# A two-attention transformer layer on one core: batches in two halves through all head pairs, with norms and FFN in portions between attention steps

## The reference, cut to what matters

```
x = x + attn_a(layernorm(x))   # 16 heads of 128, q/k/v with biases, causal softmax, w_o, b_o
x = x + ffn(layernorm(x))      # per-row int8 quantisation, one 256x256 product, scale, bias, fp16
x = x + attn_b(layernorm(x))   # 16 heads: rope on q and k, 64 slots (s, cumulative logsumexp z),
                               # ok, softmax, W2, o; rms norm, gate g*sigmoid(g), Wo
x = x + ffn(layernorm(x))      # the same FFN weights again
```

## Time and profile before

| | |
|---|---|
| median of 3 runs | 817.05 us |
| the profiled execution, its own time | 818.15 us |
| its span, first to last instruction | 816.3 us |
| granted TensorE clock, mean | 0.989 |
| TensorE busy | 783.3 us (96%) |
| VectorE / ScalarE / GpSimd busy | 579.9 / 434.7 / 285.6 us |
| read from HBM | 22.45 MB |

### The profile page before, as it was taken

One profiled execution on the slowest core, in us unless ns is written; L12 is line 12 of the kernel. 1 busy time (PEld: TensorE's weight loads), 2 busy tenths in 40 slices (PEclk: granted clock), 3 DMA queues, 4 the chain that ended last, 5 costly groups with the idle time before them and its releaser, 6 DMA issues.

```text
span 816.3 us, 14609 instructions
## 1 busy us (share of the span) xinstructions
PE 783.3 (96%) x4628; PEld 665.2 (81%) x4628; DVE 579.9 (71%) x1502; ACT 434.7 (53%) x1188; POOL 285.6 (35%) x291
## 2 busy tenths in 40 slices
PE   8999999999999996899999999999999999999975
PEld 6788888888888885578888888888888888888863
DVE  4455555545554558878887888798888788887786
ACT  3555565555546452465556466556565665665421
POOL 7211010202101004444536346355364463563222
PEclk9999999999999999999999999999999999999998
DMA  7010101101010100100101001001001010000001
GB/s 241 25 53 12 39 13 39 48 3 51 5 46 13 51 1 14 53 1 14 53 0 50 14 13 51 0 13 51 0 14 51 6 58 0 13 0 1 1 1 52
DMA packets 23654, 23.76 MB, mean 29 GB/s; under 512 B 2369, under 2 KB 23361, under 8 KB 23506
## 3 DMA queue, kind: packets, MB, share of 16 engines
q1 hardware_dynamic: 23634, 23.51, 9.0%
HBM read 22.45 MB, written 1.05 MB: 29 GB/s over the span
## 4 chain that ended last, share of the span: by engine, by line
PE 88%; DVE 7%; POOL 2%; ACT 1%; issue 1%; DMA 1%; SPq 0%; POOLq 0%; DVEq 0%; ACTq 0%
PE ps L1282 21%; PE ps L1494 11%; PE ps L1391 7%; PE ps L1289 5%; PE ps L1312 5%; PE ps L1355 3%; PE ps L1396 3%; PE ps L1506 3%; PE ps L1331 3%; PE ps L1531 3%; PE ps L1518 2%; PE ps L1548 2%; PE ps L1550 2%; PE ps L1549 2%; PE ps L1519 2%; PE ps L1520 2%
## 5 line engine op out<-in xcount | busy, mean ns | idle before, releaser
L1282 PE MATMUL ps<-xT_hi,w_hi 128*128 128x512 f32 x256 | 109.6, 428 | 2.4 <-DVE rot L1013 1.5
L1282 PE MATMUL ps<-xT_hi,w_lo 128*128 128x512 f32 x256 | 100.9, 394 | 0.0
L1282 PE MATMUL ps<-xT_lo,w_hi 128*128 128x512 f32 x256 | 100.7, 393 | 0.0
L1043 DVE TENSOR_TENSOR wt<-ps,const 128x384 f32<-128x384 f32 x128 | 68.2, 554 | 40.3 <-PE ps L1507 20.4
L384 POOL TENSOR_TENSOR w_lo<-w_raw,w_hi 128x512 fp32r<-128x512 f32 x32 | 40.8, 1284 | 157.2 <-ACT w_hi L536 155.5
L440 POOL TENSOR_TENSOR rot_s<-rot_s,const 128x512 f32<-128x512 f32 x64 | 81.9, 1291 | 20.0 <-ACT rot_s L679 20.0
L581 ACT ACTIVATE wt<-wt,negmax 128x128 f32<-128x128 f32 (+1 forms) x128 | 56.7, 444 | 28.2 <-DVE negmax L907 28.2
L895 DVE TENSOR_TENSOR v<-ps,bv_b 128x256 f32<-128x256 f32 x64 | 27.0, 422 | 51.9 <-PE ps L1289 51.9
L698 ACT ACTIVATE v<-ps 128x256 f32<-128x256 f32 x64 | 24.4, 381 | 72.5 <-PE ps L1494 72.3
L1032 DVE RECIPROCAL enz<-zs 128x128 f32<-128x128 f32 x64 | 60.3, 943 | 1.0 <-ACT zs L685 1.0
L1282 PEld LDWEIGHTS ps<-xT_hi,w_hi 128*128 128x128 f32 x256 | 48.7, 190 | 12.2 <-issue 3.5
(11 more groups left out here) (174 smaller groups left out, 2264.4 us busy)
## 6 DMA issues: line engine op xcount, KB each, us to landing
w_raw<-a_w_q SPq DMA_DIRECT2D x8, 256.0 KB, 2.5
w_raw<-a_w_k SPq DMA_DIRECT2D x8, 256.0 KB, 3.3
wv<-a_w_v SPq DMA_DIRECT2D x8, 256.0 KB, 3.4
wo<-a_w_o SPq DMA_DIRECT2D x8, 256.0 KB, 2.6
w_raw<-b_Wq SPq DMA_DIRECT2D x8, 256.0 KB, 2.5
w_raw<-b_Wk SPq DMA_DIRECT2D x8, 256.0 KB, 3.4
wc<-b_Wv SPq DMA_DIRECT2D x8, 256.0 KB, 3.4
wc<-b_Wg SPq DMA_DIRECT2D x8, 256.0 KB, 3.9
```

What stands on the lines that cost most here:

```text
L1043: d.tensor_tensor(dst, src[:, 0:384], tri3, ALU.mult).then_inc(done, 1)
L1282: ins = mm(PJ[n[0]], w[:, m, c, h * P:(h + 1) * P], x[:, c, cols], start=(t == 0), stop=(t == len(terms) - 1))
```

## The change

A phase is now half `phase // 8`, pair `phase % 8`, 16 phases (`PHASES`) of two steps each: all eight pairs for batches 0 and 1, then all eight for batches 2 and 3, in both attentions. Everything is written out; no hardware loop is left. Each pair's weights are loaded and split twice, once per half.

Attention a's second half (steps 17 to 24) carries, in portions called `middle(0, r)`, the whole passage between the attentions for batches 0 and 1. Attention b's first half (steps 1 to 8) carries the same for batches 2 and 3 (`middle(1, x)`), and its second half (steps 17 to 21) the second FFN of batches 0 and 1 (`closing`). The last phase of attention a has attention b's first tasks in place of its own next ones. All portions use bank 7, which the output groups use too; `middle_done` holds the next group until the portion has left the bank. A half's projection sums are all kept in `accT` and turned back by `sum_rows`; only the last two batches of b still use `out_proj`.

The core of the diff (each engine has its share of the portions):

```diff
+PHASES = 2 * PAIRS
+LAST = 2 * PHASES - 1
-        ffns = [Ffn("f0_", (0, 1, 6, 7)), Ffn("f1_", (0, 1, 0, 1))]
+        ffns = [Ffn("f0_", (7, 7, 7, 7)), Ffn("f1_", (7, 7, 0, 1))]
 # SyncE
-            with sp.Fori(1, PAIRS) as i:
-                sp.wait_ge(a.w_lo, a.splits * i)
-                load_qk(a, a_wq, a_wk, cols)
-                load_v(cols)
-                sp.wait_ge(a.wo_lo, i)
-                load_o(a, a_wo, cols)
+            for phase in range(2, PHASES):
+                sp.wait_ge(a.w_lo, 3 * (phase - 1) + 2)
+                load_qk(a, a_wq, a_wk, columns(phase))
+                sp.wait_ge(a.w_lo, 3 * (phase - 1) + 3)
+                load_v(columns(phase))
+                sp.wait_ge(a.wo_lo, phase - 1)
+                load_o(a, a_wo, columns(phase - 1))
...
 # GpSimd, start-up
             pool.wait_ge(norms[0].xn, 4)
             split_tail(a, 0, 0)
+            split_tail(a, 0, 1)
+            split_tail(a, 0, 2)
             ln_rsqrt(0, 2)
             ln_rsqrt(0, 3)
-            pool.wait_ge(norms[0].xn, TILES)
-            split_tail(a, 0, 1)
-            split_tail(a, 0, 2)
...
 # VectorE
+            def middle(half, r, place):
+                b = 2 * half
+                if r == 1 and place == 0:
+                    add_rows(a, b)
+                if r == 1 and place == 1:
+                    add_rows(a, b + 1)
+                if r == 1 and place == 2:
+                    ln_stats(1, b, a.fin_acc, b + 1)
+                    ln_stats(1, b + 1, a.fin_acc, b + 2)
+                if r == 2 and place == 0:
+                    ln_scale(1, b)
+                    ln_scale(1, b + 1)
+                if r == 2 and place == 2:
+                    ffn_quant(0, b)
+                    ffn_quant(0, b + 1)
+                if r == 4 and place == 0:
+                    ffn_out(0, b)
+                if r == 4 and place == 1:
+                    ffn_out(0, b + 1)
...
 # TensorE
+            def sum_rows(ph, b):
+                for t in range(2):
+                    tile = slice((2 * b + t) * P, (2 * b + t + 1) * P)
+                    for c in range(C):
+                        o = t * D + c * P
+                        ins = tr(Y_[:, o:o + P], accT[:, c, tile], ident)
+                ins.then_inc(ph.fin_ps, 1)
+            def middle(half, r, place):
+                if r in (3, 4, 6, 7, 8) and place == 0:
+                    pe.wait_ge(ph.y_acc, groups)
+                if r == 1 and place == 0:
+                    pe.wait_ge(a.y_acc, PHASES * (half + 1))
+                    sum_rows(a, b)
...
+                if r == 3 and place == 0:
+                    ffn_transpose(0, b)
+                    ffn_transpose(0, b + 1)
+                if r == 4 and place == 0:
+                    pe.wait_ge(ffns[0].qT, b + 2)
+                    ffn_product(0, b)
...
+            def a_step(x):
+                a_turn(x, 0)
+                a_task(ahead, o)
+                middle(0, r, 0)
+                a_turn(x, 1)
+                a_task(ahead, o + 1)
+                a_scores(x + 1)
+                middle(0, r, 1)
+                a_values(x)
+                a_task(ahead, o + 2)
+                if x % 2 == 1:
+                    a_task(ahead, o + 3)
+                middle_done(0, r)
...
-            ffn_product(0, 1)
-            keep_busy(4, oT_hi[:, 0, 0, :], 15)
-            transpose_x(1, 0, ffns[0].banks[0])
-            transpose_x(1, 1, ffns[0].banks[1])
-            s1_product(0)
-            s1_product(1)
-            ffn_transpose(0, 2)
...
+            x = LAST - 1
+            a_turn(x, 0)
+            b_task(0, "s")
+            a_turn(x, 1)
+            b_task(0, "q0")
+            a_scores(x + 1)
+            b_task(0, "q1")
+            a_values(x)
+            b_task(0, "z")
+            b_task(0, "k0")
+            out_group(a, x)
+            b_task(0, "k1")
...
+            for x in range(2 * PHASES):
+                b_step(x)
```

More of the change, by code:

```diff
@@ L240, in layer_kernel, with half_of, pair_of, task @@
         block = ctx.enter_context(nc.Block())
[L242 to L275, removed]
-            return bank, before + 1
-        def before_in_bank(h, j):
-            order = [(g, k) for g in (h - 1, h) for k in range(NB) if (g, k) < (h, j)]
-            return [(g, k) for g, k in order if B_BANKS[g % 2][k] == B_BANKS[h % 2][j]][-1]
+        def half_of(phase):
+            return phase // PAIRS
+        def pair_of(phase):
+            return phase % PAIRS
+        def task(phase, f):
+            n = NA * phase + f
+            return n % 2, n // 2
+        def evacuated(phase, f):
+            bank, before = task(phase, f)
+            return bank, before + 1
+        def banks_of(phase):
+            return B_FIRST if phase == 0 else B_BANKS[phase % 2]
+        def slot(phase, j):
+            bank = banks_of(phase)[j]
+            before = sum(banks_of(p).count(bank) for p in range(phase))
+            return bank, before + banks_of(phase)[:j].count(bank)
+        def slot_ps(phase, j):
+            return NB * phase + j + 1
+        def slot_done(phase, j):
+            bank, before = slot(phase, j)
+            return bank, before + 1
+        def before_in_bank(phase, j):
+            order = [(p, k) for p in range(phase + 1) for k in range(NB) if (p, k) < (phase, j)]
+            return [(p, k) for p, k in order if banks_of(p)[k] == banks_of(phase)[j]][-1]
         X_ok = X_[0][:, 0:T].rearrange("p (h t m) -> p h t m", h=2, t=2)
@@ L570, in a_qk, with closing @@
+            def closing(r):
+                if r == 3:
+                    ffn_copy(1, 0)
+                    ffn_copy(1, 1)
+            def a_qk(phase, f):
+                bank, count = task(phase, f)
+                name, half = A_TASKS[f], phase % 2
                 m, h = "qk".index(name[0]), int(name[1])
-                act.wait_ge(a.proj_ps, done)
+                act.wait_ge(a.proj_ps, NA * phase + f + 1)
                 dst = (qT, kT)[m][:, h, half * HALF:(half + 1) * HALF]
-                bias = (bqs, bk)[m][:, bass.ds(pair * 2 + h, 1)]
+                head = pair_of(phase) * 2 + h
+                bias = (bqs, bk)[m][:, head:head + 1]
@@ L663, in b_task @@
+            transposed(0, 3, 7)
+            def b_task(phase, name):
+                task_j, half = B_TASKS.index(name), phase % 2
+                bank, count = slot(phase, task_j)
+                done = slot_ps(phase, task_j)
                 tl = slice(HT * half, HT * (half + 1))
@@ L674, in b_task @@
                     behind = ROPES.index(name) - 1
-                    if not (isinstance(phase, int) and phase == 0 and behind < 1):
+                    if phase > 0 or behind >= 1:
                         act.wait_ge(b_rope, 4 * phase + behind)
@@ L1275, in proj_qk, with closing_done @@
+            def closing_done(r):
+                if r == 1:
+                    pe.wait_ge(b_.fin_acc, 2)
+                if r == 3:
+                    pe.wait_ge(ffns[1].qT, 2)
+                if r == 5:
+                    pe.wait_ge(ffns[1].y, 2)
+            def proj_qk(ph, bank, name, phase):
                 m, h = "qk".index(name[0]), int(name[1])
+                half = half_of(phase)
                 if h == 0:
-                    pe.wait_ge(ph.w_lo, pair * ph.splits + m + 1)
+                    pe.wait_ge(ph.w_lo, 3 * phase + m + 1)
@@ L1456, in b_task @@
-            def b_task(i, h, j, half, phase):
-                b_free(i, h, j)
-                name, bank = B_TASKS[j], slot(i, h, j)[0]
-                pair = i + h // 2
-                n = (bank,)
+                    pe.wait_ge(b_rotcos, 4 * p + ROPES.index(B_TASKS[k]) + 1)
+            def b_task(phase, name):
+                j = B_TASKS.index(name)
+                b_free(phase, j)
+                bank, half, rows = slot(phase, j)[0], phase % 2, half_of(phase)
+                pair = pair_of(phase)
```

1546 lines of the change are left out of this document (801 added, 745 removed).

## The result

The changed kernel is slower: 840.77 us median of 4 runs (838.3 to 842.3) against 817.4 (816.5 to 818.14) beside it, ratio 1.0284, 95% interval 1.0256 to 1.0311. The forecast was 802, with 813 as its upper end. The profiled execution is the fastest of the four (span 836.5, granted clock 0.976; the others had 0.968 to 0.972), so its steps show a little less than the median lost.

The account below looks back on a forecast made before the run. TensorE, busy 783.3 of 816.3 us, was taken as the bound. Stage terms summed to a span of 801.1 us, 15.2 under the old one, giving a forecast median of 802 us, range 786 to 813.

Parts of the forecast that it names:

- 10.5 in all: Attention b: TensorE stalls on VectorE's portions, 7.0 us in the first half plus 3.5 closing; between 0 and 29.0.
- 1.6: Whole kernel: one of the new idles lowers the clock once, costing 1.6 us (0 to 5).
- The closing's 3.5: Second half of b: stalls of 2.5 us at step 19's quantisation and 1.0 at step 21's FFN outputs.
- Start 24.0: Before the first phase: 26.4 less 0.6 for earlier w_lo and 1.8 for a wait that moves, 24.0 us.
- Portions of a 8.1: Second half of a: 5.4 us of TensorE work for portions plus 2.7 us stall on step 19's quantisation.
- Last phase of a 27.3: Last phase of a with b's first tasks: 24.3 us of work plus 3.0 of waits (0 to 7).
- End 40.4: Last phase of b and tail: 40.9 us as before, less 0.5 (0 to 4), so 40.4.
- Portions in b exposed: Attention b: all 29.0 us of VectorE's portion time shows, 820.5 us, or half the difference, 811; chance 0.12 for 810 and up.
- Doubled splits: Every phase: doubled weight splits lengthen it; at 1 us a phase 31 us more, 833 us; chance 0.05.
- The clock falls at each stall: At the stalls: three or four clock drops instead of one, 802 + 5 = 807 us; chance 0.13.
- Passage not taken away: Between a and b: b's first tasks wait on a's end, 3.0 us becomes 10, 809 us; chance 0.05.
- Portions hidden: Both attentions: stalls of 2.7, 3.0, 10.5 and the clock's 1.6 vanish, 784 us; chance 0.25 for under 793.

Follow-up runs that it names:

- spread kernel: Run 4: the changed kernel with the same portions spread over more steps, VectorE's pieces small and set where it idles, TensorE asking later; 790.72 us, ratio 0.9684.
- Run 6: The changed kernel with VectorE's lumps unmoved, but TensorE's FFN transposes, products and layer norm transposes asked for two steps later; 834.66 us, ratio 1.02.
- run 5: The changed kernel with only step 2's four xn scalings of half 1 in b moved behind the slot maxima; 838.24 us, ratio 1.0254.
- run 8: The spread kernel with only the odd steps' VectorE pieces in b moved about a microsecond earlier, ahead of the w2 masks; 801.41 us, ratio 0.9815.
- run 9: The changed kernel with ScalarE's two closing qbT copies in step 19 of b set behind the squares, no longer ahead of the first gates; 838.5 us, ratio 1.026.
- run 10: The spread kernel with 20 idle matmuls in place of 10 in the last step, in TensorE's wait for the last batch's quantized tile; 790.83 us, ratio 0.9684.
- run 1: The changed kernel with half 1's middle portions left out of b from the layer norm's statistics on; 812.35 us in one run.
- run 3: The changed kernel with GpSimd's low parts of b's weights made one column wide, so not computed; 830.67 us, ratio 1.0178.
- run 2: The changed kernel with 7 to 20 idle matmuls ahead of seven of TensorE's waits, nothing else moved; 832.99 us, ratio 1.0195.

## Why the prediction was wrong

**The step that failed is "10.5 in all", the stalls of portions in b, with the "1.6" for the clock beside it.** Portions in b were given 5.4 + 2.7 of TensorE and 10.5 of stalls, 18.6; they took 49.4. TensorE's own part was right: the spread kernel shows 9.8 with 1.1 of idle in it. Idle was 25.8 in the five steps and 2.1 in steps 18 and 21, so 27.9 where 10.5 stood, and the clock took 11.9 where 1.6 stood. The 9.6 left are TensorE's own work (8.7 by the spread kernel). Three things were missing.

- *Blocking.* The prediction saw one scaling of 1364 ns and spread its price evenly over VectorE's slack. It fell instead on the scalings ahead of the w2 masks: 4.36 for 1.6. With the splits narrow step 2 lost 5.2 us. In step 4 an addition of two SBUF tiles took 2.27 where .69 is normal, beside a low part of 2.39 on GpSimd.
- *The lump delays what is queued behind it.* The terms counted how late TensorE's own ask came (2.5 at step 3) and treated "slack of 2.35 us a step" as usable by any piece. Run 6 shows that asking later mostly renames the wait (25.0 us of idle for 27.9); runs 4, 5 and 8 show that slack is a property of a place: the same pieces cost 9.8 in the idle places and 10.7 more when some stand one place earlier, 4.3 of that because one stood ahead of its input. The upper bound, 29.0 with no slack used, held neither blocking nor clock; that the idle alone came to 27.9 is near it in part by luck.
- *Clock.* The one fall of the earlier trace rows was taken once. The stalls of steps 2, 3 and 19 brought 2.4, 2.8 and 3.2 us; filling seven stalls took 7.8 off the total.

The closing's 3.5 also missed a queue: ScalarE's copies ahead of its gates (run 9), 4.3 us with the clock.

**Other terms.** Start 24.0: 22.89. Not foreseen: step 2 of a took 12.05, because the first addition to `accT` waited for GpSimd's clearing (7.5 us of VectorE, 1.4 of TensorE idle); 10.18 in the spread kernel. Portions of a 8.1: 12.7, with the foreseen stall on qb in step 19 (3.5 for 2.7) and one on xn in step 22 (2.16) that was not. Last phase of a 27.3: 28.32. The 15 phases of b: 27.4 each and not 27.6, 3 us less in all; whether written-out steps do that or something else no run shows. End 40.4: 41.62; how much of it is the clock stays open (run 10).

Sum of the misses on the span: -1.1 + 1.9 + 4.6 + 1.0 - 3 + 30.8 + 1.2, less the 1.6 that had its own term, is 33.8; the difference is 836.5 - 801.1 = 35.4. Of the rest 1.3 lie in steps 0 to 5 of a (without step 2), which are up to .4 longer than bare ones.

**Rivals.** "Portions in b exposed" named the right place with a price of 9 to 18.5 for what was 30.8; its 29.0 was near the idle of 27.9, and what it lacked was the clock behind the stalls. "Doubled splits" ended on the right side by the wrong mechanism: they lengthen no phase (runs 1 and 3 in b; in a two bare steps of the changed kernel take 10.16 and 7.75, 17.9 as before), they only hold up the lumps. "The clock falls at each stall" was right and too cheap: 11.9 in b and 1.7 in a (step 19) for its 6.6. "Passage not taken away" did not occur. "Portions hidden" is what run 4 reaches: 790.7, where the rival's own sum was 784.

What stays open: which of TensorE's idles of 1.5 to 2.5 us lower the clock and which do not; step 6's stall, which was never changed alone; and the part of the clock in the last step.

## What to carry to other kernels

Work moved beside a loop whose TensorE is full is not paid from the other engines' mean slack but at the place where it is queued: list each idle gap of the host step, and ask of each piece who stands behind it on its engine. Keep each piece smaller than the gap, away from another engine's instructions that stretch it, and behind the inputs it needs; and put a wait for TensorE behind everything TensorE will need. Price the stalls of a full TensorE above their length: in b's portions 27.9 us of idle brought another 11.9 by the clock.

## What the runs showed of the hardware

- The same idle lowers the clock in one execution and not in the next. The 2.34 to 2.36 us wait in a's step 30 stood in all eleven profiled executions of changed kernels: the step took 14.3 to 14.4 us at a granted clock of 1.00 in seven and 15.8 to 15.95 at 0.89 in four. Such chance is in the spread of the changed kernel's four times (838.3 to 842.3), and between kernels it hides effects of 2 to 3 us: steps tell more than totals.
- VectorE's `amax` reductions (.63 to .69) were never stretched; scalings (.41) went up to 2.49 (run 2), roundings (.35) to 2.24 (run 6), additions of two SBUF tiles (.69) to 2.27, each beside a GpSimd instruction. GpSimd suffers too: in run 5 the scalings met its slot product, which took 1.54 for .74, and TensorE waited .6 for it.
